# Second FFN's receptances before its keys, and other work moved between steps of a fused scan kernel

## The reference

```python
# FFN (RWKV channel mix): xr, xk mix each token with the one before it
r = sigmoid(xr @ W_r);  k = square(relu(xk @ W_k));  out = r * (k @ W_v)
# Mamba: in-projection to xs and z (1024 channels each), causal conv of 4 taps, silu,
# x-projection to dt, B, C, and for each channel and each of 16 states:
h = exp(delta * A) * h + delta * B * xc;   y = sum_n C * h + D_skip * xc
out = (y * silu(z)) @ W_out + residual
```

## Time and profile before

| | |
|---|---|
| median of three runs | 5024.93 us (5024.33 to 5025.49) |
| the profiled execution | 5020.26 us, of which the span of its instructions is 5017.6 us |
| busy: PE, DVE, ACT, POOL | 4273.2, 4519.5, 2904.2, 3130.9 us |
| one chunk in the middle of the run (64 steps) | 300.3 us |
| mean granted TensorE clock | 0.945 of 2.4 GHz |

### The profile page before, as it was taken

The page is one execution under the profiler, slowest core; times in us unless marked ns, Lnnn a source line. Parts: engine busy times, 40 slices in busy tenths (PEclk is TensorE's granted clock), DMA queues, the critical chain, the costliest instruction groups (busy, mean ns, idle before and its releaser), DMA issues.

```text
span 5017.6 us, 57715 instructions
## 1 busy us (share of the span) xinstructions
PE 4273.2 (85%) x16640; PEld 2413.0 (48%) x16640; DVE 4519.5 (90%) x3778; ACT 2904.2 (58%) x6355; POOL 3130.9 (62%) x3200
## 2 busy tenths in 40 slices
PE   6678889898898979889898888979889898889777
PEld 2344545454554545445454454545445454554443
DVE  2799999999999999999999999999999999999982
ACT  3556656566665666656566665666656565665552
POOL 1656667576675757667575675756667575675761
PEclk9888999999999999999999999999999999999789
DMA  1546555565655656556565665656566565654651
GB/s 63 160 130 186 160 163 183 148 185 152 188 168 153 178 151 191 163 163 189 142 184 151 186 171 152 178 154 188 167 167 184 144 187 144 185 168 140 174 157 63
DMA packets 423053, 810.69 MB, mean 162 GB/s; under 512 B 41265, under 2 KB 41265, under 8 KB 418641
## 3 DMA queue, kind: packets, MB, share of 16 engines
q1 hardware_dynamic: 422736, 807.00, 56.0%
HBM read 772.25 MB, written 34.60 MB: 161 GB/s over the span
## 4 chain that ended last, share of the span: by engine, by line
PE 41%; DVE 30%; issue 14%; ACT 7%; POOL 5%; DMA 3%; DVEq 0%; SPq 0%; POOLq 0%; ACTq 0%
DVE decay L1037 13%; PE y_acc L500 9%; PE mm L416 9%; DVE g L1045 7%; PE mm L427 6%; PE mm L405 4%; PE mm L442 4%; DVE xc L997 4%; POOL dbx L1252 3%; PE mm L452 3%; PE mm L464 2%; DMA c_all<-bc_scratch 2%; PE mm L476 2%; ACT L788 1%; ACT L780 1%
## 5 line engine op out<-in xcount | busy, mean ns | idle before, releaser
L1252 POOL TENSOR_TENSOR dbx<-u,b_all 128x1024 f32<-128x1024 f32 x1024 | 2412.5, 2356 | 1475.4 <-DVE g L1045 1472.4
L1037 DVE TENSOR_TENSOR_SCAN decay<-decay,state,dbx 128x1024 f32<-128x1024 f32 x1024 | 2406.9, 2351 | 196.0 <-ACT decay L832 191.0
L500 PE MATMUL y_acc<-ident,g 128*128 128x128 f32 x8192 | 1169.2, 289 | 494.4 <-DVE g L1045 465.7
L500 PEld LDWEIGHTS y_acc<-ident,g 128*128 128x128 f32 x8192 | 994.3, 148 | 1029.8 <-DVE g L1045 724.7
L1045 DVE TENSOR_TENSOR g<-decay,c_all 128x1024 f32<-128x1024 f32 x1024 | 1244.4, 1215 | 12.2 <-issue 1.0
L829 ACT ACTIVATE decay<-delta,neg_a 128x512 f32<-128x512 f32 x1024 | 708.6, 692 | 37.7
L832 ACT ACTIVATE decay<-delta,neg_a 128x511 f32<-128x511 f32 x1024 | 686.6, 671 | 0.0
L427 PE MATMUL mm<-wbuf_c,col 128*128 128x512 f32 x1024 | 460.7, 593 | 7.8 <-ACT delta L780 7.0
L838 ACT ACTIVATE state<-decay 128x2 f32<-128x2 f32 x1024 | 168.4, 164 | 506.0 <-DVE g L1045 504.0
L997 DVE SCALAR_TENSOR_TENSOR xc<-mm,conv_sb,xc 128x509 f32<-128x509 f32 (+2 forms) x384 | 287.5, 749 | 13.6
L427 PEld LDWEIGHTS mm<-wbuf_c,col 128*128 128x128 f32 x1024 | 185.1, 190 | 198.5 <-issue 196.9
(11 more groups left out here) (98 smaller groups left out, 5379.0 us busy)
## 6 DMA issues: line engine op xcount, KB each, us to landing
b_all<-bc_scratch SPq DMA_DIRECT2D x1024, 256.0 KB, 3.9
c_all<-bc_scratch SPq DMA_DIRECT2D x1024, 256.0 KB, 4.7
wbuf_d<-in_w_r SPq DMA_DIRECT2D x32, 1024.0 KB, 8.0
wbuf_c<-in_w_v SPq DMA_DIRECT2D x32, 1024.0 KB, 8.2
xin<-in_x SPq DMA_DIRECT2D x16, 1024.0 KB, 5.4
wbuf_c<-in_w_k SPq DMA_DIRECT2D x16, 1024.0 KB, 8.5
wbuf_d<-in_w_in SPq DMA_DIRECT2D x16, 1024.0 KB, 8.1
wbuf_a<-in_w_in SPq DMA_DIRECT2D x16, 1024.0 KB, 9.6
```

Source lines behind the costliest of these rows:

```text
L500: last = pe.matmul(y_acc[:, tb, j * P:(j + 1) * P], g[:, s % PAIRS, j, tb * P:(tb + 1) * P], ident[:, :], start=n == 0 and j == 0 and tb % ...
L1037: dve.tensor_tensor_scan(d, d, flat(dbx[:, s % DBX, :, :]), state[:, batch, s, 0:1], ALU.mult, ALU.add).then_inc(scan_done, 1)
L1252: pool.tensor_tensor(dbx[:, s % DBX, :, :], u[:, q % 2, :, :], b_all[:, s % BRING, :].unsqueeze(1).broadcast_to([P, QT, W]), ALU.mult).the ...
```

## The change

In the second FFN the receptances (r) now come before the keys (k): r0 to r3 at steps 41, 42, 44, 45 and k0 to k3 at 47, 48, 51, 52, where k stood at 41, 43, 45, 46 and r at 50 to 53. The marks and the banks in `GROUPS` follow. The rest moves by step only: the residual, its store and `ffn_norm(1)` earlier (28 to 27, 29 to 28, 32 to 30), the skip columns of the last quarter later (35 to 41), the last two convolution tiles and most `conv_silu` later, the v products, dt and z4 shifted, z7 one step earlier, the load of the next input from 54 to 47, its statistics from two tiles in each of steps 58 and 59 to one in each of 51 to 54, its normalization from 63 to 58, and the mixes of both FFNs spread over more steps. No instruction is added or removed. The diff, cut to what is spoken of (left out: the lists of marks, the rest of `GROUPS`, and smaller shifts of SP's loads):

```diff
--- before.py
+++ after.py
...
-                  ("f1k0", -1, f_act[1], "rel0", 1), ("xs6", 1, m_dve, "c2_6", 0),
-                  ("f1r3", -1, f_act[1], "th3", 1), ("z4", 0, z_dve, "4", 0), ("f1v0", -1, f_dve[1], "g0", 1),
+                  ("f1k0", -1, f_act[1], "rel0", 1), ("f1k1", -1, f_act[1], "rel1", 0),
+                  ("dt0_1", 1, h_act, "xb0", 1), ("f1v0", -1, f_dve[1], "g0", 0),
...
                         sp.dma_start(wbuf["a"][:, :, :], piece(w_in, 0, 512)).then_inc(wxs_loaded[1], 16)
-                    if front and s == 29:
+                    if front and s == 28:
                         after(mark(m_act, f, "res3"))
...
-                    if scn and s == 46:
+                    if scn and s == 48:
...
-                    if ahead and s == 54:
+                    if ahead and s == 47:
...
-                    if ahead and s == 55:
+                    if ahead and s == 47:
...
                         z(it, (s - 27) // 2, slot)
-                    if front and s in (28, 30, 34, 36, 38, 40, 42, 44):
-                        xs(it, f, (28, 30, 34, 36, 38, 40, 42, 44).index(s), other)
+                    if front and s in (28, 30, 34, 36, 38, 40, 43, 46):
+                        xs(it, f, (28, 30, 34, 36, 38, 40, 43, 46).index(s), other)
                     if scn and s == 31:
...
-                    if back and s in (41, 43, 45, 46):
-                        ffn_k(it, 1, b, (41, 43, 45, 46).index(s))
-                    if front and s in (47, 48):
-                        xproj(it, f, s - 47)
-                    if scn and s == 49:
+                    if back and s in (41, 42, 44, 45):
+                        ffn_r(it, 1, b, (41, 42, 44, 45).index(s), xin)
+                    if back and s in (47, 48, 51, 52):
+                        ffn_k(it, 1, b, (47, 48, 51, 52).index(s))
+                    if front and s in (49, 50):
+                        xproj(it, f, s - 49)
+                    if scn and s == 51:
                         sum_skip(it, 3)
-                    if back and 50 <= s < 54:
-                        ffn_r(it, 1, b, s - 50, xin)
-                    if scn and s == 54:
-                        z(it, 4, slot)
-                    if back and s in (55, 57, 58, 59):
-                        ffn_v(it, 1, b, (55, 57, 58, 59).index(s))
-                    if front and s == 56:
+                    if front and s == 53:
                         dt_proj(it, f, 0, 0)
                         dt_proj(it, f, 0, 1)
-                    if scn and s in (60, 61):
-                        z(it, s - 55, slot)
-                    if scn and s == 62:
+                    if back and 54 <= s < 58:
+                        ffn_v(it, 1, b, s - 54)
+                    if scn and 58 <= s < 61:
+                        z(it, s - 54, slot)
+                    if scn and s == 61:
                         turn_y(it, it, 4)
                         turn_y(it, it, 5)
-                    if scn and s == 63:
+                    if scn and s == 62:
                         z(it, 7, slot)
...
                 act.wait_ge(f_pe[i].sem, f_pe[i].at(k, f"k{j}"))
-                act.wait_ge(f_dve[i].sem, f_dve[i].at(k, f"xr{j}"))
+                act.wait_ge(f_dve[i].sem, f_dve[i].at(k, (f"xr{j}", f"xk{j}")[i]))
                 o = col[:, j, 0:W]
...
                         mamba_columns(f, 2 * (s - 26) + 1, other)
-                    if front and s == 28:
+                    if front and s == 27:
                         make_res(f)
+                    if back and s == 30:
+                        ffn_norm(1, b, front)
+                    if scn and s in (28, 30):
+                        gate_tanh(it, s // 2 - 14)
+                    if front and s in (29, 31, 35, 37, 39, 41, 44, 47):
+                        conv_start(f, (29, 31, 35, 37, 39, 41, 44, 47).index(s), fb)
                     if scn and s == 29:
                         skip_columns(it, 2)
-                    if scn and s in (28, 30):
-                        gate_tanh(it, s // 2 - 14)
-                    if front and s in (29, 31, 35, 37, 39, 41, 43, 45):
-                        conv_start(f, (29, 31, 35, 37, 39, 41, 43, 45).index(s), fb)
-                    if back and s == 32:
-                        ffn_norm(1, b, front)
                     if scn and s in (33, 38):
...
                         lead_decay(it, 3)
-                    if scn and s == 35:
-                        skip_columns(it, 3)
                     if back and s == 36:
...
                     if back and s in (37, 38):
-                        ffn_before_k(1, b, 2 * (s - 37), front)
-                        ffn_before_k(1, b, 2 * (s - 37) + 1, front)
+                        ffn_before_r(1, b, 2 * (s - 37), xin, front)
+                        ffn_before_r(1, b, 2 * (s - 37) + 1, xin, front)
                     if back and s in (39, 40):
-                        ffn_before_r(1, b, 2 * (s - 39), xin, front)
-                        ffn_before_r(1, b, 2 * (s - 39) + 1, xin, front)
-                    if back and s in (42, 44, 46, 47):
-                        ffn_relu2(1, b, (42, 44, 46, 47).index(s))
-                    if front and s in (30, 32, 36, 38, 40, 42, 44, 46):
-                        conv_tanh(f, (30, 32, 36, 38, 40, 42, 44, 46).index(s))
+                        ffn_before_k(1, b, 2 * (s - 39), front)
+                        ffn_before_k(1, b, 2 * (s - 39) + 1, front)
+                    if scn and s == 41:
+                        skip_columns(it, 3)
+                    if back and s in (42, 43, 45, 46):
+                        ffn_tanh(1, b, (42, 43, 45, 46).index(s))
+                    if back and s in (48, 49, 52, 53):
+                        ffn_relu2(1, b, (48, 49, 52, 53).index(s))
+                    if front and s in (30, 32, 37, 38, 40, 42, 45, 48):
+                        conv_tanh(f, (30, 32, 37, 38, 40, 42, 45, 48).index(s))
                     if scn and s == 49:
                         keep_y(it, 2)
-                    if front and s == 50:
+                    if front and s == 51:
                         x_rows(f)
-                    if back and 51 <= s < 55:
-                        ffn_tanh(1, b, s - 51)
-                    if scn and s == 55:
-                        gate_tanh(it, 4)
-                    if front and s == 57:
+                    if front and s == 54:
                         softplus(f, 0, 0)
...
                         lead_decay(f, 0)
-                    if front and s == 59:
+                    if front and s == 56:
                         skip_columns(f, 0)
-                    if scn and s in (61, 62):
-                        gate_tanh(it, s - 56)
-                    if ahead and s == 63:
+                    if ahead and s == 58:
                         ffn_norm(0, it + 2)
+                    if scn and s in (59, 60, 61, 63):
+                        gate_tanh(it, (59, 60, 61, 63).index(s) + 4)
...
-                    if front and s in (4, 5):
-                        ffn_mix_k(0, f, 2 * (s - 4))
-                        ffn_mix_k(0, f, 2 * (s - 4) + 1)
+                    if front and s in (3, 4, 5):
+                        ffn_mix_k(0, f, s - 3)
+                    if front and s == 5:
+                        ffn_mix_k(0, f, 3)
                     if back and s in (6, 21, 23, 25):
                         out_add(b, (6, 21, 23, 25).index(s))
-                    if front and s in (6, 7):
-                        ffn_mix_r(0, f, 2 * (s - 6), xn_col[:, other, :, :])
-                        ffn_mix_r(0, f, 2 * (s - 6) + 1, xn_col[:, other, :, :])
-                    if back and s in (8, 22, 24, 26):
-                        out_stats(b, (8, 22, 24, 26).index(s))
+                    if front and s in (6, 7, 8):
+                        ffn_mix_r(0, f, (0, 1, 3)[s - 6], xn_col[:, other, :, :])
+                    if front and s == 7:
+                        ffn_mix_r(0, f, 2, xn_col[:, other, :, :])
+                    if back and s in (9, 22, 24, 26):
+                        out_stats(b, (9, 22, 24, 26).index(s))
...
-                    if front and s in (29, 31, 35, 37, 39, 41, 43, 45):
-                        conv_taps(f, (29, 31, 35, 37, 39, 41, 43, 45).index(s))
-                    if front and s in (33, 34, 36, 38, 40, 42, 44, 46):
-                        conv_silu(f, (33, 34, 36, 38, 40, 42, 44, 46).index(s))
-                    if back and s in (38, 39):
-                        ffn_mix_k(1, b, 2 * (s - 38))
-                        ffn_mix_k(1, b, 2 * (s - 38) + 1)
-                    if back and s in (40, 41):
-                        ffn_mix_r(1, b, 2 * (s - 40), xin)
-                        ffn_mix_r(1, b, 2 * (s - 40) + 1, xin)
-                    if scn and s == 55:
-                        gate_silu(it, 4)
-                    if back and s in (56, 58, 59, 60):
-                        ffn_gate(1, b, (56, 58, 59, 60).index(s))
```

(38 more changed lines are left out.)

54 lines of the change are left out of this document (30 added, 24 removed).

## The result

The changed kernel takes **5079.65 us** (median, 5074.07 to 5083.19), the kernel before, on the same chip, 5024.63: a ratio of 1.0109, interval 1.0092 to 1.0127. It is 55 us slower, outside the range of the prediction. The profiled execution took 5078.95 us, its span is 5076.9. Rows are read as those of before.

A forecast was written before the change was run, and what follows sets the result against it. VectorE (DVE) was taken to set the pace, PE close behind. Terms -0.7 + 0.45 + 1.3 - 2.3 + 1.8 gave +0.6 us a chunk, +8 over 14; with -3.6 and +0.7, +5: 5030 us, range 4985 to 5072.

The forecast's parts named there:

- after 9.6 us, at 2077.9 ... +1.3: Normalization at step 30 waits for the residual's store, delaying tanh and the scan of step 31: +1.3 us a chunk.
- Ring order: Store follows all of wbuf_a in its queue and lands at 2079: term +2.4, sum higher by 15 us.
- the store lands last: Slower rival: store lands after 10.9 us, term 2.7 for 1.3, 14 times, +20 us, 5050; chance 0.12.
- if the clock's low spells move: Listed sign that the prediction is wrong: DVE's waits change outside the named places; no size given.
- Residual a step earlier: Decay of step 28 ends later behind the residual, so its scan waits 0 to 1.0 us: +0.45 a chunk.
- First FFN's mixes: Steps 3 to 9: PE's sum of step 7 and the groups after it come sooner: -0.7 us a chunk.
- Second FFN's head: Steps 35 to 38: waits for conv_tanh and xs3 shrink, the xs6 wait goes: -2.3 us a chunk.
- the keys: Keys behind receptances, steps 47 to 55: longer chain to the scan of step 52: +1.8 us a chunk.
- predicted gap of 2.4: PE stands about 2.4 us before step 48's sum, for relu, square and keep_y.
- clock rival: Slower rival: granted clock falls in the gap before step 48's sum, +1.8 a chunk, +25 us, 5055; chance 0.18.
- Start and end: Once per run: earlier input load and statistics give -3.6 us; v0's longer wait at the end costs +0.7.
- clock rival with a late store: Low clock before step 48's sum combined with a late store; put at 5070, the range's slow side.

The follow-up runs named there:

- e4: Kernel before with only the residual (step 27), its store (28) and the second FFN's normalization (30) moved; 5068.33 us, ratio 1.0095.
- e1: Changed kernel with the second FFN's normalization put back to ACT's step 32; 5021.66 us, ratio to before 1.0004.
- e2: Changed kernel with the residual's store one step later, at SP's step 29, normalization staying at step 30; 5121.26 us, ratio 1.0202.
- e6: Changed kernel with the load of wbuf_a issued at step 29, behind the residual's store, instead of step 27; 5031.90 us, ratio 1.0024.
- e15: e1 with 16 more transposes on PE at the end of step 31, filling idle time; step 33 is 1.73 us shorter than in e1.
- e13: Kernel before with only the first FFN's mixes and step 8's statistics moved (steps 3 to 9); 5020.77 us, ratio 1.0000.
- e3: Changed kernel with ACT's keep_y of step 49 ahead of relu and square of k1; 5040.75 us, ratio 1.0042.
- e12: e1 with PE's group of z2 ahead of the sum of g in step 32; the median moves by 2 us against e1.
- e14: Kernel before with 16 more transposes on PE at the end of step 31, filling idle time; 25 us faster.
- e7: Changed kernel with normalization back at step 32 and keep_y of step 49 ahead of relu and square of k1; 4981.36 us, ratio 0.9920.
- e8: Kernel before with one extra VectorE instruction (128x512) in step 27 of each scanned chunk; 1 us slower than before.
- e16: Kernel before with one extra VectorE instruction (128x512) in step 30 of each scanned chunk; 7 us slower than before.
- e9: Kernel before with three extra VectorE instructions (128x512) in step 27 of each scanned chunk; 14 or 21 us slower (text does not say which).
- e17: Kernel before with two extra VectorE instructions (128x512) in step 30 of each scanned chunk; 14 or 21 us slower (text does not say which).

## Why the prediction was wrong, point by point

- **The failed step** is the size of "after 9.6 us, at 2077.9 ... +1.3": the store took 11.3 us and the term is 3.3. I took the landing of `wbuf_a` for that of a store that stands behind `wbuf_a` in the same queue. The rows of a load alone, or of the first of two, say nothing on the second. Ring order, worked out there to 2079 and +2.4, was nearer, and still short; it left out the loads of B and C that stand between the two as well. The mechanism was right in each link (ACT stopped, the tanh behind it, DVE waiting), and the rival "the store lands last", given a chance of 0.12, is the case that came, at 3.3 instead of 2.7. e4 shows it alone, e1 removes it, e2 doubles it, e6 and the packets give its cause.
- **Where the rest is.** With 3.3 for 1.3 the sum is +2.6 a chunk, 36 us, 5058. The other 0.8 a chunk, 11 us, is the longer wait for z2 at step 33, which the prediction did not have at all ("if the clock's low spells move" was its only mention). e1 shows that the stall does not cause it; e15 that the low clock after the idle time does. What is left, some 10 us, lies at the edges and in the third scanned chunk (307.2 us), which no term covered.
- **Residual a step earlier, +0.45**: measured 0.00; the scan of step 28 waits 0.12, its product comes 0.21 later, and step 29 is shorter by the same 0.21, since an instruction there is held up for less time (last section). A delay ahead of a wait is no loss.
- **First FFN's mixes, -0.7**: right by luck. The mixes alone gave nothing (e13); 0.46 stand at step 0, which lost a gate.
- **Second FFN's head, -2.3, and the keys, +1.8**: steps 36 to 63 come to +0.07 against -0.5, and the two terms were not measured apart. The predicted gap of 2.4 is 2.41, the wait at the scan of step 52 2.52 for 2.5, the others 0.99 and 1.12 for 0.8 and 1.2. The clock rival did not come: granted 1.00 across the gap.
- **Start and end**: -2.5 for -3.6; v0's wait +0.57 for +0.7; the other edges were put at nothing and cost 10.
- **Slips in the working.** The parts named for the store's term, 0.6 and "another half us", make 1.1 and not 1.3; 15.9 + 0.7 + 1.7 is 18.3 and not 18.4; and the clock rival with a late store is 5075, not 5070. None of them would have brought the measured time into the range.

**Still open.** Twelve kernels have chunks that stand, for many chunks on end, at 297.0, 300.4, 303.8 or 307.1 us, and moves of 0.2 to 0.8 us vanish between them: the changed parts that sum to -0.9 outside steps 32 to 35 (e1), the +0.2 of e13, doses of 0.4 and 0.7. Other kernels (e3, e12, e14, e15) wander between these values, so they are no law. The four values are equally far apart, 3.4 us each time, and the change's 3.42 a chunk is just one such distance: the prices read here in steps 30 and 31 (from 2.3 to 3.8 in single chunks of the changed kernel) and after them add up to it in nearly every chunk. Where a kernel stands, its granted clock falls at the same place of each chunk, in before 159.2 to 159.4 us after the chunk's first product and in e1 160.3, in all ten chunks; in e3, which wanders, at 162.2 to 165.8. So the low spells and the chunk are in step. Which of the two draws the other, why these values, and why a chunk returns to them, is not shown; that the low clock has a part is shown at z2 alone.

## What to carry to other kernels

A transfer that an engine waits for also pays for what stands ahead of it in its queue: before moving a store earlier, count the bytes issued before it, not the landing of a neighbour. A wait put in front of in-order work prices everything behind it; here one 2.9 us normalization, moved two steps ahead, cost 3.3 us in each of 14 chunks, and moving it back gave all of it. Where the pacing engine waits behind a matmul group that follows idle time, try filling or closing that gap before shifting vector work: one moved group gave 46 us on the kernel before, more than the change with both its repairs (40). It is no sure gain: the same move gave 2 us on e1. And when a loop's duration does not move by an edit, look at the steps before calling the edit worthless: a gain can be there and be taken back elsewhere (e1), and come out with the next edit (e7).

## What the runs showed that I had not expected

The middle chunks' duration is stiff against small edits (e8, e13, e16). And the same extra instruction, 128x512 from SBUF to SBUF, took 1.65 us on average in step 27 (e8) and 0.70 in step 30 (e16). In step 27 it starts 0.9 us into a product of GpSimd and ends just after it:

```profile
2065.00 2.35 POOL L1264 TENSOR_TENSOR dbx<-u,b_all 128x1024 f32<-128x1024 f32 x1
2065.90 1.74 DVE L962 TENSOR_SCALAR pad<-ident 128x512 f32<-128x512 f32 x1
```

The Trainium skill ("Trainium Architecture — The Big Picture", What this means for kernel authors) says that VectorE and GpSimd share a pair of SBUF ports under an exclusive lock. The row agrees, and so do all the others: in e8, e9, e16 and e17 each such instruction in the loop that meets a product ends 0.28 or 0.29 us after the product's end, whether it then took 0.64 or 2.6. Each one that meets none takes 0.43, as do the second and third in e9's step 27. Not every VectorE instruction is held: the 1024 scans keep 2.34 to 2.36 us, products or not.

The same thing is the slack of step 29. Its first convolution instruction works on 3 columns, which elsewhere takes 0.15 us. In before it starts 1.0 us into a product and ends 0.02 after it; in e9 (the last row below), where DVE comes later, it starts 0.1 us before the product's end and takes 0.15. The 1.2 us between the two count as busy time and as no wait, and they are what swallows a delay ahead of them (e8, e9, and the residual of the change).

```profile
2072.21 2.36 POOL L1252 TENSOR_TENSOR dbx<-u,b_all 128x1024 f32<-128x1024 f32 x1
2073.23 1.37 DVE L989 TENSOR_TENSOR xc<-xc,head 128x3 f32<-128x3 f32 x1
...
2092.31 0.15 DVE L997 TENSOR_TENSOR xc<-xc,head 128x3 f32<-128x3 f32 x1
```
